# A second mixture of experts in which the first gate and up pair of the next chunk or expert is issued ahead of the present down product

## What is computed

```python
xn = xf * rsqrt(mean(xf * xf, -1) + eps)
probs = softmax(xn @ router_w.T)               # 8 experts, the best 2 for each token
topk_p, topk_i = top_k(probs, 2)
rw = topk_p / topk_p.sum(-1, keepdims=True)
capacity = int(1.25 * 2048 / 8)                # 320 rows for each expert
xg = xf[dispatch]                              # [8, 320, 128], rows of each expert in order of tokens
gate = silu(einsum('ech,ehi->eci', xg, rg))    # 128 -> 512
up = einsum('ech,ehi->eci', xg, ru)
eout = einsum('eci,eih->ech', gate * up, rd)   # 512 -> 128
routed = zeros.at[dispatch].add(eout * weight)
shared = silu(x @ sg) * (x @ su) @ sd          # 128 -> 1024 -> 128, for all tokens
return shared + routed
```

## Time and profile before

| | us |
|---|---|
| three runs, median (lowest, highest) | 1408.36 (1408.22, 1408.46) |
| profiled execution, span of its instructions | 1427.8 |
| second mixture in it, from barrier to barrier | 425 to 604.7 |
| one chunk of the shared expert (chunk 2) | 22.75 |
| one routed expert | 8.95 and 9.10 in turn |

### The profile page before, as it was taken

One profiled execution on the slowest core, in us unless ns is written; L12 is line 12 of the kernel. 1 busy time (PEld: TensorE's weight loads), 2 busy tenths in 40 slices (PEclk: granted clock), 3 DMA queues, 4 the chain that ended last, 5 costly groups with the idle time before them and its releaser, 6 DMA issues. The chain is left out here.

```text
span 1427.8 us, 21449 instructions
## 1 busy us (share of the span) xinstructions
PE 1234.0 (86%) x6427; PEld 612.9 (43%) x6427; DVE 1133.5 (79%) x1639; ACT 1042.2 (73%) x1809; POOL 960.0 (67%) x916
## 2 busy tenths in 40 slices
PE   6377599999628999898999999999999999999876
PEld 3361144444415566634444444444444444444332
DVE  6857599999676222248999999999999999999996
ACT  3337599999452223269889999998999899989871
POOL 7651411111463623238999999999999999999985
PEclk9786799999859999999999999999999999999987
DMA  2022223333218103244143414341444243414410
GB/s 65 20 92 77 81 81 114 109 121 98 60 35 301 48 19 121 74 116 106 47 105 90 114 50 95 89 118 55 97 93 101 61 108 89 96 50 105 92 52 15
DMA packets 89708, 123.56 MB, mean 87 GB/s; under 512 B 17141, under 2 KB 48576, under 8 KB 89224
## 3 DMA queue, kind: packets, MB, share of 16 engines
q1 hardware_dynamic: 83048, 103.92, 27.3%
q0 software_dynamic: 6560, 18.44, 4.3%
HBM read 96.18 MB, written 26.92 MB: 86 GB/s over the span
## 5 line engine op out<-in xcount | busy, mean ns | idle before, releaser
L2304 DVE TENSOR_TENSOR_SCAN hs<-decay,dbx 128x512 f32<-128x512 f32 x512 | 589.0, 1203 | 21.2 <-ACT decay L2187 6.8
L1871 POOL TENSOR_TENSOR hcm<-hs,Cc 128x1024 f32<-128x1024 f32 x192 | 453.2, 2371 | 20.4 <-DVE hs L2304 11.9
L2187 ACT ACTIVATE decay<-dtr,a_cur 128x512 f32<-128x512 f32 x512 | 351.9, 712 | 11.0 <-DVE hs L2304 10.7
L1992 PEld LDWEIGHTS dbx<-ident_sb,scaled 128*128 128x128 f32 x1536 | 175.9, 141 | 258.2 <-DVE hs L2304 137.4
L1992 PE MATMUL dbx<-ident_sb,scaled 128*128 128x128 f32 x1536 | 238.7, 280 | 34.7 <-DVE hs L2304 33.5
L2165 ACT ACTIVATE scaled<-duT,BT 128x256 f32<-128x256 f32 x506 | 224.9, 497 | 10.3 <-PE dbx L1992 10.3
L1864 POOL TENSOR_TENSOR hck<-hs,Cc 128x512 f32<-128x512 f32 x128 | 164.1, 1282 | 36.3 <-DVE hs L2304 36.3
L1989 PE MATMUL dbx<-du,spread_sb 128*128 128x512 f32 x256 | 140.2, 630 | 2.8 <-DVE hs L2304 2.8
L921 ACT ACTIVATE ex<-tt 128x1024 f32<-128x1024 f32 x128 | 137.2, 1072 | 6.1 <-DVE tt L971 5.0
L1919 PE MATMUL slots<-XT,w_tap 128*128 128x512 f32 (+1 forms) x240 | 123.3, 601 | 2.3 <-PEq L1311 2.3
L1854 POOL TENSOR_SCALAR scaled<-duT,BT 128x256 f32<-128x256 f32 x256 | 118.6, 489 | 0.0
(11 more groups left out here) (348 smaller groups left out, 2018.9 us busy)
## 6 DMA issues: line engine op xcount, KB each, us to landing
dtr<-dt_turn SPq DMA_DIRECT2D x60, 512.0 KB, 8.5
Cc<-bc_turn SPq DMA_DIRECT2D x256, 64.0 KB, 2.0
dt_turn<-dt SPq DMA_DIRECT2D x15, 512.0 KB, 2.8
Bb<-bc_turn SPq DMA_DIRECT2D x64, 64.0 KB, 2.0
conv_row<-in_conv_row SPq DMA_DIRECT2D x4, 512.0 KB, 5.8
shares_of_tokens<-zeros SPq DMA_DIRECT2D x2, 1024.0 KB, 9.7
w_rg<-in_w_rg SPq DMA_DIRECT2D x8, 256.0 KB
w_ru<-in_w_ru SPq DMA_DIRECT2D x8, 256.0 KB
```

The costliest lines, as they stand in the source:

```text
L1871: nc.gpsimd.tensor_tensor(hcm[:, (m - 1) % MR:m % MR + 1, :], hs[:, q % HR:p % HR + 1:p - q, :], Cc[:, k:k + 1, :].broadcast_to([P, 2, 512 ...
L1992: last = nc.tensor.transpose(dbx[bank_of[p]][:, P * kk:P * kk + P], scaled[:, (b + k) % 2, kk, g, :, :].rearrange("p j c -> p (j c)"), ide ...
L2187: nc.scalar.activation(dec[:, p % DR, :], dtr[:, b % 2, g, :], ACT.Exp, scale=a_cur[:, 4 * g + k:4 * g + k + 1]).then_inc(s_dec, 1)
L2304: nc.vector.tensor_tensor_scan(hs[:, p % HR, :], dec[:, p % DR, :], dbx[bank_of[p]][:, :], 0.0, ALU.mult, ALU.add).then_inc(s_sc, 1)
```

## The change

Three things are written in another order, on TensorE and on ScalarE alike; VectorE, GpSimd and SyncE keep their programs.

- Shared expert: the pair f = 0 of chunk c + 1 is issued after the pair f = 7 of chunk c (in chunk 0 after the two ranking products) and ahead of the down product of chunk c. Chunks 1 and 2 are turns of a loop, chunk 3 is written out.
- Routed experts: the pair f = 0 of the next expert is issued after the pair f = 3 of the present one and ahead of its down product, with its waits for the turned rows and for the weights.
- The rows of the next expert are turned behind the pair f = 1 and no longer behind f = 3.

The core of the diff (ScalarE's program is moved in the same way: SiLU of the moved pair ahead of the copy of the down product):

```diff
+                    shared(1, range(1))
                     shared_down(0)
-                    with pe.Fori(1, 4) as c:
-                        shared(c)
+                    with pe.Fori(1, 3) as c:
+                        shared(c, range(1, 8))
+                        shared(c + 1, range(1))
                         shared_down(c)
+                    shared(3, range(1, 8))
+                    shared_down(3)
...
+                    def gate_up(q, i, f):
+                        if f == 0:
+                            pe.wait_ge(s_tc, at(q, 2, i + 1))
+                            pe.wait_ge(s_w8[i], q * 48 + 48)
+                        pe.wait_ge(s_hd8, at(q, 8, 4 * i + f - 1))
+                        mm(g_bank[f % 2][:, 0:CAP], w_rg[i][:, P * f:P * f + P], xgT[:, i, :], start=True, stop=True)
+                        mm(u_bank[f % 2][:, 0:CAP], w_ru[i][:, P * f:P * f + P], xgT[:, i, :], start=True, stop=True).then_inc(s_gu8, 1)
+
                     def experts(q, more):
                         for i in range(2):
...
+                            gate_up(q, i, 1)
                             if i == 0:
                                 turn_rows(q, 1)
                             elif more:
                                 turn_rows(q + 1, 0)
+                            gate_up(q, i, 2)
+                            gate_up(q, i, 3)
+                            if i == 0:
+                                gate_up(q, 1, 0)
+                            elif more:
+                                gate_up(q + 1, 0, 0)
                             pe.wait_ge(s_hd8, n(4, 4))
```

More of the change, by code:

```diff
@@ L1430, in _, with shared @@
                     pe.wait_ge(s_w4, 16 * 3)
-                    def shared(c):
-                        for f in range(8):
+                    def shared(c, fs):
+                        for f in fs:
                             pe.wait_ge(s_hd, at(c, 8, f - 1))
@@ L1444, in shared_down @@
                         last.then_inc(s_od, 1)
-                    shared(0)
+                    shared(0, range(8))
                     pe.wait_ge(s_clr, 10)
@@ L1489, in _ @@
                     turn_rows(0, 0)
+                    gate_up(0, 0, 0)
                     with pe.Fori(0, 3) as q:
@@ L1505, in shared, with keep_shared @@
                             nc.scalar.activation(sil[:, f % 2, :], g_bank[f % 2][:, :], ACT.Silu).then_inc(s_si, 1)
+                    def keep_shared(c):
                         act.wait_ge(s_od, at(c, 1, 1))
                         nc.scalar.activation(GATE[:, bass.ds(c * 4, 4), :], o_bank[:, :, :], ACT.Copy).then_inc(s_oc, 1)
-                    shared(0)
-                    with act.Fori(1, 4) as c:
-                        shared(c)
+                    shared(0, range(8))
+                    shared(1, range(1))
+                    keep_shared(0)
+                    with act.Fori(1, 3) as c:
+                        shared(c, range(1, 8))
+                        shared(c + 1, range(1))
+                        keep_shared(c)
+                    shared(3, range(1, 8))
+                    keep_shared(3)
                     def keep_rows(q, i):
@@ L1515, in keep_rows, with gate8 @@
                         nc.scalar.activation(xgT[:, i, :], x_bank[:, 0:CAP], ACT.Copy).then_inc(s_tc, 1)
+                    def gate8(q, i, f):
+                        act.wait_ge(s_gu8, at(q, 8, 4 * i + f + 1))
+                        act.wait_ge(s_hd8, at(q, 8, 4 * i + f - 1))
+                        nc.scalar.activation(sil[:, f % 2, 0:CAP], g_bank[f % 2][:, 0:CAP], ACT.Silu).then_inc(s_si8, 1)
                     def experts(q, more):
@@ L1519, in experts @@
                             n = lambda per, k: at(q, 2 * per, i * per + k)
[L1520 to L1523, removed]
+                            gate8(q, i, 1)
                             if i == 0:
@@ L1527, in experts @@
                                 keep_rows(q + 1, 0)
+                            gate8(q, i, 2)
+                            gate8(q, i, 3)
+                            if i == 0:
+                                gate8(q, 1, 0)
+                            elif more:
+                                gate8(q + 1, 0, 0)
                             act.wait_ge(s_ed, n(1, 1))
@@ L1536, in _ @@
                     keep_rows(0, 0)
+                    gate8(0, 0, 0)
                     with act.Fori(0, 3) as q:
```

## The result

The changed kernel takes 1415.01 us (median of six runs, 1412.31 to 1418.84), the kernel before beside it 1408.62 (1408.22 to 1411.45): ratio 1.004, interval 1.0021 to 1.0058. The forecast was 1408.5 with a range up to 1412.0, so it is slower than I said and outside the range. In a second comparison on another chip the ratio was 1.0019, 0.9998 to 1.0039. Both say: no gain, and a few us slower, 5.6 and 2.7 by the two ratios; the interval of the second alone just includes 1.

A forecast was written before the change was run, and what follows sets the result against it. TensorE, the busy engine, was taken to bound the second mixture of experts, its idle moving the time. Shared part - 4.4 and routed part + 4.5 gave + 0.1 us, hence 1408.5 us, range 1404.8 to 1412.0.

The forecast's parts named there:

- shared part: Shared expert: moved pairs fill TensorE's hole ahead of the down products of chunks 0 to 2, - 4.4 us.
- six periods of the ring: Routed experts, loads of experts 2 to 7: waiting for weights lengthens four periods by 2.6 us together, two by 2.5.
- first period: Routed experts, first period, weights asked early: gets the moved pair, loses its last hole; 9.4 against 9.12 us, + 0.3.
- last expert and end: Last routed expert: its first pair is already done, so its down product ends at T + 8.15 instead of 9.0, - 0.85 us.
- Rival 3: Routed experts: weights do not hold the moved pair, 8.35 us in all six periods, 1399.4 us in all; chance 0.07.
- the ring's period: Routed experts: weight landing, release, moved pair and down product add to 9.67 us, 10.22 for the last two periods.
- From the last packet to the waiting engine I take 0.4 us: Routed experts: time from a weight load's last packet to TensorE's start, taken from a GpSimd wait for conv_row.
- The weights then land at T + 5.1: Routed experts: loads of experts 2 to 5 complete 5.1 us after T, those of 6 and 7 after 5.65.
- T: Routed experts: the moment when an expert's down product ends and the next TensorE instruction starts.
- Rival 1: Routed experts: row loads asked earlier crowd the weight loads, 3 to 3.5 us slower, 1411.4 to 1412.0; chance 0.18.
- Rival 2: Routed experts: weights reach TensorE sooner, release 0.1 us and last loads like the first, 1405.6 us; chance 0.16.
- rival 4: Written-out chunk or a changed clock at the stage's end costs something no row prices, within + 2 us; chance 0.04.

The follow-up runs named there:

- e1: Kernel before with only the shared expert's pairs moved, the routed experts written as before; ratio 0.9949 to the kernel before.
- e2: Kernel before with only the routed experts in the new order, the shared expert written as before; ratio 1.0072 to the kernel before.
- e10: Changed kernel with gate and up weights asked after the expert's fourth pair, w_rd after its down product, one wait for all three; ratio 0.9924 to the kernel before.
- e5: Changed kernel with next-row loads and GpSimd's sends home both held until the expert weights asked before them have landed; ratio 1.0010 to the kernel before.
- e4: Changed kernel with only the loads of the next rows held until the expert weights asked before them have landed; ratio 1.0025 to the kernel before.
- e7: Kernel before with GpSimd's three sends home of expert 6 moved behind the barrier and SyncE's last wait not covering them; ratio 0.9994 to the kernel before.
- e6: Changed kernel with e10's early asks, and the moved pair waiting only for gate and up weights, the down product for w_rd; ratio 0.9919 to the kernel before.
- e8: e6 with the sends home of expert 6 also moved behind the barrier, as in e7; ratio 0.9884 to the kernel before.
- e11: Changed kernel with only GpSimd's sends home held until the weights asked just before them have landed; ratio 1.0041 to the kernel before.

## Why the prediction was wrong

The sum, term by term, on the mixture of the first profiles:

| term | forecast | measured | from |
|---|---|---|---|
| shared part | - 4.4 | - 5.3 | 97.98 against 103.26 |
| six periods of the ring | + 5.1 | + 7.8 | 61.80 against 54.02 |
| first period | + 0.3 | - 0.1 | 10.50 against 10.58 |
| last expert and end | - 0.85 | 0.0 | 11.29 against 11.30 |
| sum | + 0.1 | + 2.4 | 181.57 - 179.16 |

**The mechanism was right, the size of its main term was not.** The moved pair waits for weights, the wait closes a ring through the down product, the copy and SyncE, and it eats the shared gain. e1, e2 and e10 show it from three sides: the gain alone, the loss alone, and the loss turned into a gain when only the asks are moved. Rival 3 (weights that don't hold, 8.35 us a period) is what e10 makes true, with 8.2; in the change as made it is not.

**The failed step is the size of the ring's period.** I wrote 9.67 us four times and 10.22 twice, 59.1 in all; it was 61.8 (61.7 in the second profile), + 2.7. Its pieces, over six loads:

- "From the last packet to the waiting engine I take 0.4 us": by the packets' records the last packet of w_rd starts 26.1 us after the asks in sum (26.3 in the second profile), and TensorE starts after 30.1 (30.0): 0.62 to 0.67 a load, between 0.4 and 0.9. That is + 1.3 to + 1.6. I had read it from one case, on GpSimd.
- "The weights then land at T + 5.1": from ask to last packet I had 3.96, and 4.5 for the last two, 24.9 in sum; it was 26.1 (26.3). That is + 1.2 to + 1.4. e5 points to other traffic: with none beside, asks to starts take 27.7 us, about the 27.2 of the forecast. The kernel before has the same sends beside its loads and 4.07 (4.13 in its second profile) from ask to last packet; what is new beside them are the row loads, yet holding the rows alone brings back little. Which of the two makes the loads slower than before stays open.
- The ask itself: I took 1.14 us after T from one period. It is 1.14 and 1.27 in turn, in the earlier trace rows already (540.69 - 539.42 = 1.27): + 0.4.
- From the moved pair to the end of the down product it is 4.07 us (527.31 - 523.24) where I took 4.17: - 0.6.

The last load is not slower than the first ones here (4.3 and 4.4 us for the last, 4.7 and 4.9 for the first): what I read from the earlier trace rows was scatter. In the second profile of the kernel before the last load takes 4.1 and the second one 4.7.

**The last expert's 0.85 was no gain**, since I let TensorE close the mixture. Its last down product does start 1.2 us sooner after T (583.14 - 578.36 against 599.39 - 593.44), but the next stage waits for GpSimd. I had called GpSimd under a third busy; in the chunk that the earlier trace rows shows it is busy 11.19 of 22.75 us. The rows of the end (GpSimd's last send, 5.96 us, next stage) stood in the trace of before and I didn't look at who closes the block.

**The shared part** was right in kind and 0.7 to 0.9 too small. Down products are 20.96 us apart where I had 22.76 - 1.64 = 21.12; in the last chunk the hole shrank from 1.88 to 1.41, the 0.4 I had left at zero; chunk 0 is 0.75 late for the 0.59 forecast. hid's single buffer costs nothing, as I said. The forecast of the mixture is off by 2.3 us only because the shared part and the first period (1.3 together) made up for part of the ring and the end (3.55): luck, not accuracy.

**Rivals.** Rival 1 named the right side and the wrong mechanism: rows alone are worth 0.5 us of the ring (e4), not 3. The rule of the Trainium skill, DMA: Bandwidth & Descriptors, section "Queues, rings and completion order", that on each DMA engine one ring's descriptors are consumed in order, agrees with e4 (29.6 against 30.1 from asks to starts), though a difference of this size could be chance. Rival 2 had the release at 0.1, and it was 0.64.

**The rest of the time.** The ring explains why the mixture is 2.4 to 2.8 us longer. Added to the kernel before that is about 1411, still inside my range; the first comparison has 5.6 to 6.4 us. The other 3 to 4 lie outside the mixture, where the forecast had nothing but rival 4's + 2, and the range nothing for the scatter of the untouched stages. The runs show what goes with that scatter. In each of the four later jobs the runs of the kernel before are the longer the lower their mean granted clock is (correlation - 0.84 to - 0.89), by 0.9 to 1.3 us for each 0.001. Compared at the same mean clock, with straight lines of one slope through the runs of both kernels of a job (an estimate from them, bounds of 95%), the changed kernel is 3.0 us slower in the second comparison (1.6 to 4.4), e7 0.9 faster, e10 10.9, e6 10.5 and e8 12.6 (11.0 to 14.2): within 2 us of what their mixtures say. The others agree as well, e1 the worst (7.3 against 5.0 to 5.3). Of e8's 16 us about 4 go with the clock: its runs had 0.949 in the mean and those beside them 0.944. No run sets the clock, so that it is the cause is a reading and not shown.

**What stays open.** For the first comparison the clocks of the kernel before are not on record, so its surplus over the mixture can't be put down to the clock by numbers; six runs of the kernel before within 3.2 us were also fewer and closer than the 18 of a later job, which spread over 9.7. Open too are what moves the mean clock from run to run, and which traffic slows the loads.

## What to carry over

When a step is moved ahead of another to fill a hole, look for the slowest thing among its own waits, and ask whether what now stands behind it is what releases that thing: then a slack of some us becomes a ring, and each of its pieces (ask, load, release) counts in full every turn. Move the ask along with its user: the same order of products with its loads asked as soon as the buffers are really free went from 1.0019 to 0.9924. And before a gain at the end of a block is counted, see which engine closes the block. Where two runs differ by more than the changed stage does, look at their granted clock first.

## What the chip showed beyond that

- From the start of the last packet of a load to TensorE's start with it: 0.4 to 0.9 us, 0.64 in the mean of the twelve loads in the two profiles of the changed kernel.
- Three loads of 262 KB asked within 0.9 us take 3.8 to 4.9 us from the first ask to the last packet, 4.35 in the mean; with all other traffic held (e5), 4.0.
- GpSimd's next stage starts 5.96 us after its last indirect DMA of the block has been issued, in both kernels, and 5.97 in e11 where that DMA was 0.65 us later. 4.39 us of it are a drain that starts when the DMA has landed, the same in the twelve profiles whose block ends with such a send; in e7 and e8 it takes 4.14 and is hidden.
- A fall of the granted clock to 0.50 turned a down product of 2.9 us into one of 4.5 (e2), after a wait of 1.96 us; after waits of 2.57 and 2.67 at the same place (the changed kernel) it did not fall.
- The stretch behind the mixture, the same instructions, took 825.75 and 822.2 us in two profiles of the changed kernel, so a single pair of profiles can't show a difference of 3 us there. The stretch in front of it took 425.58 and 402.35 us in two profiles of the kernel before, at a mean clock of 0.86 and 0.89.
